# ScalarE in place of SyncE issues the stores of the split queries and keys

## What is computed

```
xn = layernorm(x)
cp = leaky_relu(xn @ Wc.T + bc)            # 256 + 1024 columns
q, k = cp[:, :128], cp[:, 128:256]         # 16 heads of 8
v = cp[:, 256:]                            # 16 heads of 64
s = xn + leaky_relu(softmax(q k / sqrt 8) v @ Wo.T + bo)
g = silu(mixture of 8 experts, 2 per token, of xn)
x = x + s * g
```

## Time and profile before

| | us |
|---|---|
| median of 3 runs | 1372.5 |
| lowest, highest | 1370.63, 1372.51 |
| the profiled execution, its own time | 1366.37 |
| its span | 1364.6 |
| mean granted clock | 0.911 |

### The profile page before, as it was taken

The page is one execution under the profiler, slowest core; times in us unless marked ns, Lnnn a source line. Parts: engine busy times, 40 slices in busy tenths (PEclk is TensorE's granted clock), DMA queues, the critical chain, the costliest instruction groups (busy, mean ns, idle before and its releaser), DMA issues.

```text
span 1364.6 us, 14825 instructions
## 1 busy us (share of the span) xinstructions
PE 1067.8 (78%) x4798; PEld 496.4 (36%) x4798; DVE 913.7 (67%) x1475; ACT 551.5 (40%) x813; POOL 718.2 (53%) x523
## 2 busy tenths in 40 slices
PE   4868957995799998999888878589866355669887
PEld 2346644121121222222111156467543121257574
DVE  5746726885688888888987547576766477764423
ACT  2533313564566665656565523112221101354242
POOL 4440042788688878888899901331333546550402
PEclk9979988998799999999999979799997666789999
DMA  6456652111110101010001324344310102022451
GB/s 212 147 161 199 197 159 61 51 30 41 28 42 18 42 18 42 17 43 21 14 29 31 111 88 150 103 143 139 97 33 12 31 16 96 26 75 85 151 161 54
DMA packets 100113, 108.21 MB, mean 79 GB/s; under 512 B 22860, under 2 KB 76748, under 8 KB 100036
## 3 DMA queue, kind: packets, MB, share of 16 engines
q1 hardware_dynamic: 86500, 96.41, 22.9%
q0 software_dynamic: 5120, 10.50, 2.5%
q10 hardware_dynamic: 8416, 0.36, 0.3%
HBM read 78.84 MB, written 27.92 MB: 78 GB/s over the span
## 4 chain that ended last, share of the span: by engine, by line
PE 43%; DVE 18%; POOL 16%; issue 8%; ACT 5%; another core or an unknown queue 3%; DMA 2%; ACTq 2%; SPq 1%; POOLq 0%; DVEq 0%
PE ps L141 39%; POOL psum_sb L147 7%; PE ps L144 4%; POOL ar L147 3%; ACT ar L184 3%; DVE ar L160 3%; DVE ar L147 3%; DVE small L160 2%; DVE osb L160 2%; ACTq L187 2%; DVE ps_sb L147 1%; POOL gT L197 1%; SPq L187 1%; POOL acc_sb L197 1%
## 5 line engine op out<-in xcount | busy, mean ns | idle before, releaser
L141 PE MATMUL ps<-ar 128*64 128x512 f32 (+3 forms) x3052 | 679.8, 477 | 67.2 <-ACT ar L184 39.8
L141 PEld LDWEIGHTS ps<-ar 128*64 128x64 f32 (+2 forms) x3052 | 278.6, 144 | 430.1 <-issue 266.8
L184 ACT ACTIVATE ar<-ps 128x1024 f32<-128x1024 f32 (+2 forms) x318 | 303.8, 961 | 222.8 <-PE ps L141 167.1
L160 DVE TENSOR_REDUCE small<-ps 128x2 f32<-128x1024 f32 (+2 forms) x276 | 310.4, 1142 | 53.1 <-PE ps L141 51.3
L147 POOL TENSOR_TENSOR psum_sb<-psum_sb,ar 128x1024 f32<-128x1024 f32 x128 | 306.4, 2394 | 19.8 <-ACT ar L184 5.0
L147 POOL TENSOR_TENSOR ar<-ar 128x256 f32<-128x256 f32 (+1 forms) x32 | 96.2, 3021 | 95.6 <-DVE ar L160 93.4
L147 POOL TENSOR_TENSOR psum_sb<-ar 128x1024 f32<-128x1024 f32 x32 | 76.1, 2378 | 62.8 <-ACT ar L184 50.9
L197 POOL DMA_INDIRECT gT<-ysort,rt x48 | 46.2, 962 | 113.6 <-issue 113.6
L181 ACT COPY ar<-ps 128x256 f32<-128x256 f32 (+1 forms) x72 | 27.3, 385 | 169.9 <-PE ps L144 121.4
L147 DVE TENSOR_TENSOR ar<-ps,ar 128x256 f32<-128x256 f32 (+4 forms) x62 | 58.8, 955 | 43.4 <-ACT ar L181 13.7
L147 DVE TENSOR_TENSOR ar<-ar,ps 128x512 f32<-128x512 f32 (+1 forms) x70 | 55.8, 799 | 47.2 <-PE ps L141 22.6
(11 more groups left out here) (151 smaller groups left out, 1245.6 us busy)
## 6 DMA issues: line engine op xcount, KB each, us to landing
ar<-in_L_w SPq DMA_DIRECT2D x30, 576.0 KB
ar<-in_L_w SPq DMA_DIRECT2D x22, 578.0 KB
ar<-in_L_w SPq DMA_DIRECT2D x30, 384.0 KB
rec_sb<-lscr SPq DMA_DIRECT2D x64, 128.0 KB
ar<-xsort SPq DMA_DIRECT2D x52, 128.0 KB
ysort<-ar SPq DMA_DIRECT2D x52, 128.0 KB
scr<-ar SPq DMA_DIRECT2D x48, 128.0 KB, 2.1
osb<-xsort SPq DMA_DIRECT2D x30, 128.0 KB
```

Source lines behind the costliest of these rows:

```text
L141: return self.e.matmul(o, l, r, start=start, stop=stop) if self.e else Nothing()
L160: return self.e.tensor_reduce(o, a, AX.X, op, negate=True) if negate else self.e.tensor_reduce(o, a, AX.X, op)
L184: return self.e.activation(o, a, fn, **kw) if self.e else Nothing()
```

## The change

The stage `qk` leaves SyncE's program. In ScalarE's, `qk` gets a seventh step: after its third cast it yields once, waits for that cast and for the zeros, and issues the same six or eight stores.

```diff
@@ scalar_program, qk @@
                 if k < 2:
                     yield
                     yield
+            yield
+            act.wait_ge(*at("qk_act", c, ty, 2))
+            act.wait_ge(*at("zeros", 0))
+            name = f"scr_out{k4}"
+            for r, which in enumerate((QORD, KORD)[ty]):
+                act.dma(scr[ty, r, :, cols(c)], pt[which]).then_inc(
+                    *landed((name, c, ty) if ty == 1 and r == 5 else (name,)))
+            if ty == 0:
+                for q in range(2):
+                    o_ = CW * c + 256 * q
+                    act.dma(scr[ty, 6, :, o_:o_ + 256], zero_b).then_inc(*landed((name, c, ty) if q else (name,)))
@@ sync_program @@
-        def qk(c, ty):
-            k4 = (2 * c + ty) % 4
-            o_ = 1024 + 768 * k4
-            pt = [parts[:, o_ + 256 * i:o_ + 256 * i + 256].bitcast(BF16) for i in range(3)]
-            for _ in range(6):
-                yield
-            sp.wait_ge(*at("qk_act", c, ty, 2))
-            sp.wait_ge(*at("zeros", 0))
-...
-        stages = {"qk": qk, "max0": max0, "tail0": tail0, "l3start": l3start, "end3": end3, "first": first}
+        stages = {"max0": max0, "tail0": tail0, "l3start": l3start, "end3": end3, "first": first}
```

## The result

| | before | after |
|---|---|---|
| median, us | 1370.98 (9 runs, 1369.26 to 1372.51) | 1378.68 (9 runs, 1372.26 to 1382.35) |
| the profiled execution, its own time | 1366.37 | 1379.98 |
| its span | 1364.6 | 1378.2 |
| mean granted clock | 0.911 | 0.909 |

The ratio is 1.0060, 95% interval 1.0041 to 1.0079: the change costs 5.6 to 10.8 us, 7.7 between the medians. The two profiled executions lie 13.6 us apart, so a difference of two traces can overstate the cost by some microseconds; I use the traces for places and the medians for sizes.

What follows compares the result with a forecast made beforehand. Bound taken: TensorE full in the v projection, then the ACT-DVE routing chain and unexplained stands. Block costs less 0.6 gained sum to 2.2 or 5.9 us; middle 4 gives 1376 us, range 1373.5 to 1380 (8 in 10: 1363 to 1385).

Steps and rivals of the forecast that it cites:

- two sums, 2.2 and 5.9: Net loss over all blocks less 0.6 us gained on SyncE: 2.2 at 0.50 us an issue, 5.9 at 0.60.
- ScalarE issues at SyncE's price: Each store issued on ScalarE costs 0.50 us with the gap, as on SyncE; 0.60 was the dearer case.
- issues in a burst are dear: Rival: 14 issues inside POOL's scatters cost 1.6 us each, 15 us more, about 1387 us; chance 0.08.
- (0,0) and the six-blocks nearly free: (0,0) costs 0.1 us; (1,1), (2,1), (3,1) inside moe cost 0 to 0.9 in all, taken as 0.3.
- (0,1) and (1,0), taken as 2.0 to 3.0: Blocks stored during and after the v projection: together 2.0 us at 0.50 an issue, 3.0 at 0.60.
- TensorE's first loss: Block (0,1) in the v projection delays a bank's release; TensorE, never idle there, loses 1.9 us near 53 us.
- 1.7 us, with the backlog of (0,1) 2.0: DVE's second routing step at 64.15 comes 1.7 us later through (1,0), 2.0 us with the backlog of (0,1).
- the wait of 2.46 us for the first sorted rows: TensorE's wait before 65.64, set by POOL's scatters: covers TensorE's own loss, but not the DVE chain behind the routing.
- (2,0), taken as 0.3, with 0.6 gained on SyncE: Eight-block in moe: costs 0.3 us at 0.50 an issue; freeing SyncE of stores gains 0.6 us.
- The load that I said would come 4 us early: SyncE's load of sorted rows at 115.28 starts at about 111.3 once the eight stores of (2,0) are gone.
- The unexplained pieces shrink: Rival: TensorE's stands before 95.48 and 204.03 shrink by 9.6 us, giving 1367 us; chance 0.30.
- Hidden anyway: Rival: ACT's delay is swallowed by TensorE's wait until 65.64 and the burst-bound stands, giving 1373 us; chance 0.22.

Runs made afterwards that it cites:

- e2: ScalarE stores all blocks but (0,1) and (1,0), which SyncE stores; against the kernel before: 1323.65 us, ratio 1.0041.
- e7: Like e2, but from (1,1) on issues are spread, two per slot for (1,1), one for the others; against e5: 1364.30 us, ratio 1.0010.
- e12: ScalarE stores block (2,0) alone, SyncE the other seven; against the kernel before: 1322.34 us against 1319.07, ratio 1.0016.
- e6: The changed kernel, unchanged, run again on the chip of e5; against the kernel before: 1372.64 us against 1363.22, ratio 1.0064.
- e5: The kernel before, unchanged, run again on one chip with e6, e7 and e8 as their base: 1363.22 us.
- e1: ScalarE stores only blocks (0,1) and (1,0), SyncE the other six; against the kernel before: 1323.29 us against 1317.78, ratio 1.0039.
- e4: Kernel before with all stores on SyncE, first sorted-row loads and their wait put behind the stores of (0,1) and (1,0): 1319.84 us, ratio 1.0014.
- e10: ScalarE stores block (0,1) alone, SyncE the other seven; against the kernel before: 1319.86 us against 1319.07, ratio 1.0003.
- e11: ScalarE stores block (1,0) alone, SyncE the other seven; against the kernel before: 1318.40 us against 1319.07, ratio 0.9996.
- e3: Kernel before with SyncE's stores kept, plus as many tiny 128 x 8 stores issued by ScalarE at the change's places: 1336.85 us, ratio 1.0135.
- e8: Changed kernel with repeated parts stored by one DMA each, three or four issues instead of six, same bytes; against e5: 1370.71 us, ratio 1.0059.
- e9: Kernel before, all stores on SyncE, stack's eight loads moved from slot 41 to slot 39: 1318.67 us against 1319.07, ratio 0.9997.

## Why the prediction was right in sign and short in size

The forecast was 4 us slower; it was 7.7. The 4 was the middle between two sums, 2.2 and 5.9, and the cost lies above both. That 1376 lies within 3 us of the measured 1378.68 is in part luck: the kernel before came out 1.5 us faster (1370.98) than the 1372.5 that I had added to. Step by step:

- **ScalarE issues at SyncE's price: right.** ScalarE's 48 stores have a median of 480 ns, SyncE's had 456; the blocks take 2.84 to 3.69 us for six. The dearest of the 48 is 1307 ns (at 49.6, with no issue of SyncE beside it), and the rival "issues in a burst are dear" falls: the block in the burst that took longest, 3.69 us, is 0.61 each.
- **(0,0) and the six-blocks nearly free: not separated.** e2 costs 5.4 us, of which (2,0) alone is 2.1; the remaining 3.3 (with an interval of over 2 us either way) of (0,0), (1,1), (2,1), (3,0), (3,1) was forecast as 0.1 + 0.3 + 0.1. e7 shows that it is gone when the stores are spread, with (0,0) still in one piece, so (0,0) is nearly free as forecast. Whether the other four cost anything stays open; in the traces e2 stands only 0.35 us behind e12.
- **(0,1) and (1,0), taken as 2.0 to 3.0: the term that was mis-sized.** TensorE's first loss was right (1.9 forecast; 2.05, 1.65 and 1.85 measured). The step that failed is "1.7 us, with the backlog of (0,1) 2.0": I let the two delays overlap at the routing step, but TensorE was full before it, so the first loss is carried into the second block and they add, 5.8 us (e6 against e5, 65.33 to 71.13) and 5.6 (e1 against e4, 60.58 to 66.20), which is e10's 2.6 plus e11's 3.0; even alone (1,0) delays the step by 3.0 and not 1.7. I also had the cover at the wrong place: the wait of 2.46 us for the first sorted rows did not leave the routing chain exposed. With one block the routing step is 2.6 to 3.0 us late and the time is unchanged; with both, the excess over the cover is what counts. That is shown on chips without the "remote" stands; on those with them the traces differ (7.0 us left at the tile behind the second burst in the pair of the result, 1.0 in e6 against e5).
- **(2,0), taken as 0.3, with 0.6 gained on SyncE: wrong in sign.** The load that I said would come 4 us early was not the one TensorE waits for. I priced the stores as issue time on two queues and left out that on ScalarE they start ahead of a load that in SyncE's order they followed. Measured +2.1 us (0.5 to 3.8) in e12. Of this price 1.4 us in e12's trace is TensorE at the lower clock behind the longer wait, a term that the sum did not have at all. On issues that meet one of the other engine: SyncE's load takes 0.77 us instead of 0.42 and ScalarE's store beside it 0.99 instead of 0.48 (e12, at 95.5 and 95.7). The rule that I weighed is from the Trainium skill, "Perfetto Trace Analysis", section on the HWDGE DMA instruction: the descriptor generator is locked for exclusive use, and the wait for it lies inside the profiled time. These two issues agree with it, and so may the one pair of the earlier trace rows with 808 and 1599 ns, whose other fifteen show nothing. But a single long issue is no proof of a meeting, as the 1.41 us above and the 1307 ns of ScalarE show, both with nothing beside them. At most 0.35 us of the load that TensorE waits for is the meeting. The larger part, 1.7 us more from the end of the issue to TensorE's start, is not issue time, and the rule does not tell it. What holds the load up there stays open; it happens without the bytes of the stores too (e3).
- **The unexplained pieces shrink: not in the result, and open beyond it.** The stand before the second burst's end is 12.41 us where it was 12.36; the later ones did not go (6.35 and 4.82 us before 205 and 214 us in the profile after, 4.89 and 5.50 before 193 and 204 in that of before). On the second chip with such stands the first is shorter in all three kernels that move stores (8.72, 10.09 and 8.69 us in e6, e7 and e8, against 12.15 in e5) and the later ones are not; the time fell in none. What sets these stands is not shown. On the chips of e1 to e4 and e9 to e12 the same kernel has neither.
- **Hidden anyway: half right.** It is just what each of the first two blocks does alone, and what spreading does for the others.

What stays open beside the above: e8's small return, the half of e1's cost that has no place in its trace, and how the 7.7 us divide on a chip with "remote" stands, where no block was moved alone.

## What to carry to other kernels

A wait that covers one delay covers it once: when several moved pieces lie ahead of the same wait, add up their losses first and subtract the cover last, and try them together, since each alone may show nothing. Price a longer wait of TensorE with the work behind it: here the tile after it took 1.4 to 2.8 us more at the lower clock in all six traces where the stores had made the wait longer, and in two where they had not. A DMA handed to another engine also takes another place among the DMAs; look at which load was in front of it and whether somebody waits for that load. If an engine with little slack must issue many DMAs, one or two behind each of its computations were free here; six or eight in a row were free only where a later wait covered them.

## What the hardware showed beside this

- The same kernel took 1363 to 1371 us on some chips and 1318 to 1319 on others. The traces of the latter have none of the "remote" stands of ScalarE and VectorE during POOL's indirect transfers; the 12 us before 95 us are replaced by a wait of 1.0 us.
- After some of TensorE's idles its pairs of matmuls took 2.06 us instead of 1.02 for a while, at half clock (1.2 GHz). The length of the idle alone does not tell when: 1.59 us was followed by 2.08 (e11), 1.85 us by 1.12 (e10). At the wait for sorted rows in (2,0) the tile behind ran at a mean granted clock of 1.00 after 2.93 us and less (e1, e4, e5, e7, e11 and the kernel before), at 0.55 to 0.71 after 3.30 us and more (seven traces), and at 0.70 after 1.68 us (e9).
- The kernel before has a mean granted clock of 1.00 from 60 to 80 us in one profile and 0.83 in another (e5), so the clock's part of the 7.7 us can't be given from single traces; at (2,0) it is 1.5 us in the pair of the result.
- An issue goes by instruction, not by bytes: 1.56 us for three stores that carry what six carried in 3.10.
